# Two-layer graph network on one core: TensorE runs further ahead in the second layer, and the first layer's additions stand two groups later

## The reference, cut to what matters

```python
    edge_index = jnp.stack([src, dst])
    h = jnp.maximum(_layernorm(x, axis=-1), 0.0)
    x = x + _L0_gnn_ref(h, edge_index, L0_gnn_kernel, L0_gnn_bias)
    h = jnp.maximum(_layernorm(x, axis=-1), 0.0)
    x = x + _L1_gnn_ref(h, edge_index, L1_gnn_Wq, L1_gnn_bq, L1_gnn_Wk, L1_gnn_bk, L1_gnn_Wv, L1_gnn_bv, L1_gnn_gamma, L1_gnn_beta)
```

```python
        sums = jax.ops.segment_sum(msg, row, num_segments=n)
        cnt = jax.ops.segment_sum(jnp.ones_like(ew), row, num_segments=n)
        reduced = sums / jnp.maximum(cnt, 1.0)[:, None]
        h = jnp.concatenate([reduced, x], axis=1) @ kernel + bias
        return jax.nn.relu(h)
```

```python
        att = jnp.einsum('ehd,ehd->eh', q, k) / jnp.sqrt(jnp.float32(HEAD_DIM))
        exp_att = jnp.exp(jnp.clip(att, -10.0, 10.0))
        att_sum = jax.ops.segment_sum(exp_att, rows, num_segments=num_nodes)
        att_norm = exp_att / (att_sum[rows] + 1e-08)
        weighted_v = (att_norm[..., None] * v).reshape(-1, D_MODEL)
        out = jax.ops.segment_sum(weighted_v, rows, num_segments=num_nodes)
```

## Time and profile before

| | us |
|---|---|
| median of 3 runs | 6205.74 (6203.47 to 6215.74) |
| the profiled execution | 6258.93 |
| its span | 6257.2 |
| PE busy | 3015.3 (48%) |
| DVE busy | 3094.1 (49%) |
| ACT busy | 1816.7 (29%) |
| POOL busy | 3185.1 (51%) |

### The profile page before, as it was taken

How to read it: one execution, slowest core, us unless ns; L and a number is a source line. 1 busy time by engine, 2 the same in 40 slices (tenths; PEclk the granted TensorE clock), 3 DMA queues, 4 the chain that set the end, 5 groups by cost and what they waited for, 6 DMA issues and landing times. The chain is left out here.

```text
span 6257.2 us, 86473 instructions
## 1 busy us (share of the span) xinstructions
PE 3015.3 (48%) x21028; PEld 2368.1 (38%) x21028; DVE 3094.1 (49%) x8514; ACT 1816.7 (29%) x5489; POOL 3185.1 (51%) x3338
## 2 busy tenths in 40 slices
PE   4445445445445445344465555554554545445453
PEld 3323323333333233233243444444444444444442
DVE  6536445445445445344244555555555555555556
ACT  3233332333332333333443222222222222222222
POOL 4364464464463464554535555555555555555554
PEclk8555555556556555555557666666666666666666
DMA  2231231231222221222322222222222222222223
GB/s 80 54 82 47 64 82 46 67 79 48 70 74 50 73 73 49 76 70 62 73 54 75 76 75 75 76 76 76 76 76 76 76 76 75 76 76 75 75 76 56
DMA packets 205061, 436.91 MB, mean 70 GB/s; under 512 B 67172, under 2 KB 114781, under 8 KB 204606
## 3 DMA queue, kind: packets, MB, share of 16 engines
q0 software_dynamic: 153968, 371.50, 22.4%
q1 hardware_dynamic: 49934, 59.56, 3.4%
q10 hardware_dynamic: 704, 0.33, 0.0%
HBM read 415.27 MB, written 55.69 MB: 75 GB/s over the span
## 5 line engine op out<-in xcount | busy, mean ns | idle before, releaser
L525 POOL DMA_INDIRECT got<-hk_table,dst x1563 | 1523.3, 975 | 1513.1 <-PE bank L1000 821.5
L1486 POOL DMA_INDIRECT kv<-kv_table,dst_i x1611 | 1527.0, 948 | 1287.6 <-DVE wv_s L1528 846.8
L766 DVE TENSOR_TENSOR acc<-acc,bank 128x129 f32 x2187 | 635.3, 290 | 1480.8 <-remote 737.7
L1633 PE MATMUL bank<-q,ohT 128*128 x4833 | 617.9, 281 | 934.5 <-ACT ohT L1585 834.0
L998 PE MATMUL bank<-got,oh 128*128 x2187 | 616.9, 285 | 794.5 <-issue 445.1
L1644 PE MATMUL bank<-wv_s,oh_f 128*128 128x136 f32 x3222 | 768.5, 397 | 463.9 <-DVE wv_s L1528 249.8
L1507 DVE TENSOR_TENSOR prod<-bank,kv 128x384 f32<-128x384 f32 x537 | 297.7, 554 | 1271.6 <-remote 1042.3
L1633 PEld LDWEIGHTS bank<-q,ohT 128*128 128x128 bf16 x4833 | 481.7, 121 | 1035.1 <-issue 985.8
L1644 PEld LDWEIGHTS bank<-wv_s,oh_f 128*128 128x128 f32 x3222 | 635.2, 279 | 536.0 <-DVE wv_s L1528 297.9
L1579 ACT ACTIVATE oh_f<-oh 128x384 f32<-128x384 bf16 x537 | 279.6, 521 | 1683.0 <-remote 1235.2
L1101 ACT ACTIVATE oh<-away 128x384 bf16<-128x384 bf16 x733 | 383.8, 524 | 1311.5 <-remote 788.0
(11 more groups left out here) (223 smaller groups left out, 3409.3 us busy)
## 6 DMA issues: line engine op xcount, KB each, us to landing
slots_by_bin<-sorted_chunk SPq DMA_DIRECT2D x637, 61.0 KB
kv<-kv_table,dst_i POOLq DMA_INDIRECT x1611
got<-hk_table,dst POOLq DMA_INDIRECT x1563
kv_table<-qkv SPq DMA_DIRECT2D x12, 512.0 KB, 2.9
hk_table<-hk POOLq DMA_DIRECT2D x6, 772.0 KB, 5.7
out<-o SPq DMA_DIRECT2D x12, 256.0 KB
xs<-in_x SPq DMA_DIRECT2D x3, 768.0 KB, 10.7
sorted_chunk<-vT SPq DMA_DIRECT2D x13, 64.0 KB
```

The lines of the kernel that those rows point to most:

```text
L525: g.indirect_dma_start(out=got[:, (tile0[k] + t) % RING0, :], out_offset=None, in_=hk_d, in_offset=bass.IndirectOffsetOnAxis(dst0[:, k % 2 ...
L766: v.tensor_tensor(out=o, in0=o, in1=bank[5 + u % 3][:, i * W0:(i + 1) * W0], op=ALU.add)\
L1486: g.indirect_dma_start(out=kv[:, r, i, :], out_offset=None, in_=kv_d, in_offset=bass.IndirectOffsetOnAxis(dst_i[:, t:t + 1], 0))\
L1633: ins = t.matmul(bank[2 + u % 2][:, i * D:(i + 1) * D], ohT[:, u % 2, i * P:(i + 1) * P], q3[:, bass.ds(regs[0][(s + i) % REGS], 1), j * D ...
```

## The change

In the second layer all distances of PE grow by one or two groups: the transposes stand 4 groups ahead instead of 2, the queries 3 instead of 1, and the sums 2 behind instead of 1. PSUM's banks are shared anew: the transposes have one bank (0) instead of two, the queries three (1 to 3) instead of two, the sums keep two (4, 5). The one-hot matrices on DVE are made 5 groups ahead instead of 3, the widening and the eviction on ACT stand 4 ahead instead of 2, and the buffers `oh_f`, `ohT` and `wv_s` are twice as deep. DVE's additions stay 3 groups behind. In the first layer DVE adds the group two earlier (`LAG0`), with the placing steps where they were; the last two groups are added behind the loop.

```diff
@@ first layer, DVE
+                groups = [(i, g) for i in range(CHUNKS) for g in range(groups0(i))]
                 for k in range(1, CHUNKS + 1):
...
-                        if g < groups0(k - 1):
-                            add(k - 1, g)
+                        if g < groups0(k - 1) and group0[k - 1] + g >= LAG0:
+                            add(*groups[group0[k - 1] + g - LAG0])
...
+                for k, g in groups[-LAG0:]:
+                    add(k, g)
@@ second layer, buffers
-        oh_f = sbp(phase, "oh_f", [P, 4, G, P], FP32)
-        ohT = sbp(phase, "ohT", [P, 2, G * P], BF16)
+        oh_f = sbp(phase, "oh_f", [P, 8, G, P], FP32)
+        ohT = sbp(phase, "ohT", [P, 4, G * P], BF16)
...
-        wv_s = sbp(phase, "wv_s", [P, 2, G, W], FP32)
+        wv_s = sbp(phase, "wv_s", [P, 4, G, W], FP32)
@@ DVE, weigh
-                    if u >= 2:
-                        v.wait_ge(s_s, u - 1)
+                    if u >= 4:
+                        v.wait_ge(s_s, u - 3)
@@ DVE, the loop
-                    if u + 3 < GROUPS:
-                        hot(u + 3)
+                    if u + 5 < GROUPS:
+                        hot(u + 5)
@@ ACT, widen and the loop
-                    if u >= 4:
-                        a.wait_ge(s_s, u - 3)
+                    if u >= 8:
+                        a.wait_ge(s_s, u - 7)
...
-                    if u + 2 < GROUPS:
-                        widen(u + 2)
-                        evict(u + 2)
+                    if u + 4 < GROUPS:
+                        widen(u + 4)
+                        evict(u + 4)
@@ PE, turn
-                    if u >= 2:
-                        t.wait_ge(s_oT, u - 1)
+                    if u:
+                        t.wait_ge(s_oT, u)
@@ PE, queries
-                    if u >= 2:
-                        t.wait_ge(s_prod, u - 1)
+                    if u >= 3:
+                        t.wait_ge(s_prod, u - 2)
@@ PE, the loop
-                for u in range(GROUPS + 1):
-                    if u + 2 < GROUPS:
-                        turn(u + 2)
-                    if u + 1 < GROUPS:
-                        queries(u + 1)
-                    if u:
-                        sums(u - 1)
+                for u in range(GROUPS + 2):
+                    if u + 4 < GROUPS:
+                        turn(u + 4)
+                    if u + 3 < GROUPS:
+                        queries(u + 3)
+                    if u >= 2:
+                        sums(u - 2)
```

More of the change, by code:

```diff
@@ L1525, in weigh @@
                     v.wait_ge(s_exp, u + 1)
[L1526 to L1528 removed]
+                    if u >= 4:
+                        v.wait_ge(s_s, u - 3)
+                    v.tensor_tensor(out=by_head(wv_s[:, u % 4, :, 0:D]),
                                     in0=by_head(kv[:, u % RING1, :, D:2 * D]),
@@ L1549, in _ @@
                 v.wait_ge(s_i1, 1)
-                for u in range(3):
+                for u in range(5):
                     hot(u)
@@ L1576, in widen @@
                     a.wait_ge(s_o1, u + 1)
-                    if u >= 4:
-                        a.wait_ge(s_s, u - 3)
-                    a.activation(oh_f[:, u % 4, :, :], oh1[:, u % 4, :, :], ACT.Copy).then_inc(s_of, 1)
+                    if u >= 8:
+                        a.wait_ge(s_s, u - 7)
+                    a.activation(oh_f[:, u % 8, :, :], oh1[:, u % 4, :, :], ACT.Copy).then_inc(s_of, 1)
                 def evict(u):
                     a.wait_ge(s_tt, u + 1)
-                    if u >= 2:
-                        a.wait_ge(s_q, u - 1)
-                    a.activation(ohT[:, u % 2, :], bank[u % 2][:, :].bitcast(BF16)[:, 0:G * P], ACT.Copy)\
+                    if u >= 4:
+                        a.wait_ge(s_q, u - 3)
+                    a.activation(ohT[:, u % 4, :], bank[0][:, :].bitcast(BF16)[:, 0:G * P], ACT.Copy)\
                      .then_inc(s_oT, 1)
@@ L1591, in expo @@
                         a.wait_ge(s_wgh, u)
-                    if u >= 2:
-                        a.wait_ge(s_s, u - 1)
-                    a.activation(wv_s[:, u % 2, :, D:W], att[:, u % 2, :, :], ACT.Exp,
+                    if u >= 4:
+                        a.wait_ge(s_s, u - 3)
+                    a.activation(wv_s[:, u % 4, :, D:W], att[:, u % 2, :, :], ACT.Exp,
                                  scale=float(HEAD_DIM) ** -0.5)
@@ L1597, in expo @@
                      .then_inc(s_exp, 1)
-                for u in range(2):
+                for u in range(4):
                     widen(u)
@@ L1643, in sums @@
                     for i in range(G):
-                        ins = t.matmul(bank[4 + u % 2][:, i * W:(i + 1) * W], oh_f[:, u % 4, i, :],
-                                       wv_s[:, u % 2, i, :], start=True, stop=True)
+                        ins = t.matmul(bank[4 + u % 2][:, i * W:(i + 1) * W], oh_f[:, u % 8, i, :],
+                                       wv_s[:, u % 4, i, :], start=True, stop=True)
                     ins.then_inc(s_s, 1)
                 turn(0)
-                turn(1)
-                queries(0)
-                for u in range(GROUPS + 1):
-                    if u + 2 < GROUPS:
-                        turn(u + 2)
-                    if u + 1 < GROUPS:
-                        queries(u + 1)
-                    if u:
-                        sums(u - 1)
+                for u in range(3):
+                    turn(u + 1)
+                    queries(u)
+                for u in range(GROUPS + 2):
[5 more added lines that the diff above has]
+                        sums(u - 2)
     layer1.close()
```

9 lines of the change are left out of this document (4 added, 5 removed).

## The result

The changed kernel takes 6119.35 us (median of 4 runs, 6104.86 to 6125.97) against 6210.54 (6203.47 to 6215.74) for the kernel before: ratio 0.9851, 95% interval 0.9829 to 0.9872. It is 91 us faster; 6444 had been forecast, slower. The time lies in the stated range of 6030 to 6590, but only because that range was drawn down to rival A's end; the forecast's own range was 6260 to 6590. It lies near rival A's 6095.

What follows compares the result with a forecast made beforehand. It took the second layer to be bound by a ring of waits in which PE's signals are held while gathers land. The median 6205.74 plus 263 (second layer) minus 25 (first layer) gave 6444 us, range 6030 to 6590, its own 6260 to 6590.

Steps and rivals of the forecast that it cites:

- rival A: Second layer: sums slip through, rounds keep three groups and only the restart is shorter; −86, 6095 us; chance 0.15.
- What bounds the kernel: Second layer: while a train's gathers land, PE's signals are held and come together 2.97 us after its last gather.
- Step 2: Second layer: queries 3 ahead take away the product's 1042 us wait, but only as far as DVE's additions allow.
- Step 3: Second layer: sums lose one iteration of slack and are held, so rounds carry two groups instead of three; +263 us.
- rival B: Second layer: signals late by a fixed delay, hidden by look-ahead, POOL the bound; −809, 5372 us; 0.13 with what lies toward A.
- Step 1 and 4: Second layer: transposes 4 ahead in one bank, taken as 0; deeper buffers opening the held sum's detour, 0 beside the round.
- First layer: First layer: additions two groups later let placing work fill DVE's waits for sums; −25 us, bounds −91 to +123.
- two upper bounds, +387 and +123: Second layer if the restart stays at 2.60 us, +387; first layer if PE's waits for additions double, +123.

Runs made afterwards that it cites:

- a1_second: The change's second layer alone, with the first layer's additions as in the kernel before: 4594.67 us, ratio 1.0001, on a chip with prompt signals.
- c1_lag1: The kernel before with the first layer's additions one group behind, old second layer: 6176.83 us, ratio 0.9935, on the chip with held signals.
- d3: Changed second layer with sums one behind, old first layer, each PE signal passed through a small DMA: 4815.34 us, ratio 1.0487 to the kernel before.
- d4: Changed second layer with sums two behind, old first layer, each PE signal passed through a small DMA: 5065.37 us, ratio 1.1024 to the kernel before.
- a2_first: The change's first layer alone, all second-layer edits undone: 4559.38 us, ratio 0.9916 to the kernel before, prompt signals.
- b2_adds4: The changed kernel with second-layer additions 4 groups behind instead of 3, three banks for sums, two for queries: 4559.48 us, ratio 0.9915 to the kernel before.
- a3_sums1: The changed kernel with the second layer's sums one group behind instead of two: 4554.89 us, ratio 0.9918 to the kernel before, prompt signals.
- a4_deep: The kernel before with only the deeper buffers, all distances unchanged: 4596.96 us, ratio 1.0003, prompt signals.

## Why the prediction was wrong, point by point

**What bounds the kernel: right for its chip, but for one reading.** Trains of nine gathers, held signals, a release 3 us after the last gather: all is in the trace after as in the one before. That the held signals "come together" is not so: in the earlier trace rows the held sums pass at 5007.03, 2.2 us before the product's signal, and over all trains the fourth signal comes at a median of 10.7 us into the train, the fifth at 12.9. As a statement on gathers it is too wide: on chips with prompt signals the same rows land without a pause and PE's signals are never late. There the Trainium skill's rule (SBUF — State Buffer, section Who interferes with whom) and the trace agree: in a1_second PE's signals come at a median of 0.01 us after the modelled end while rows land. On the chip with held signals no run tells whether the rule fails or something else holds the signals. Nor does a run tell whether the signals alone are late or the matmuls too, since a matmul's recorded end is modelled.

**Step 2, the queries' look-ahead: right.** The product's wait is gone (1042.3 to 2.5 us), DVE stands at the addition at the release, and POOL starts 2.13 us after it instead of 2.60. These are single rounds: times the 179 rounds of nine gathers the 0.47 us make 84 us, close to the 86 that the second layer gained, and partly by luck. The mean over all trains is 2.55 us before (and in c1_lag1) and 2.15 after, 0.40 us or some 70 us in all; the rest is that the release comes a little sooner, by the mean 3.07 us after the last gather in c1_lag1 and 2.96 us after it in the changed kernel.

**Step 3, the sum's lost iteration: the wait was right, the price was wrong, and this is the step that failed.** The wait at the additions came (1169 us), but not its price: −86 us were measured in the second layer where +263 had been forecast. The price of 263 us rested on "3.4 is nearer to the held one, so I take them as held": sums that end 3.4 us after the train's start were taken as held, because in the earlier trace rows sums that ended at 4.13 were. In the round above they end 3.75 us after the start (4745.89 + 1.70 against 4743.84), and the addition at 4748.15 follows 0.56 us later. In another round of the changed kernel they end 5.13 us after the start, later than the held ones of the earlier trace rows, and still pass within 0.2 us:

```profile
4758.94 0.95 POOL L1491 DMA_INDIRECT kv<-kv_table,dst_i  x1 [4.14 <-DVE wv_s L1533]
...
4762.37 1.70 PE L1649 MATMUL bank<-wv_s,oh_f 128*128 128x136 f32 x6
...
4764.21 0.30 DVE L1551 TENSOR_TENSOR acc<-acc,bank 128x136 f32 x1 [1.91 <-issue]
```

So the time from the train's start does not decide. (The profile marks this wait "issue", since the record of this signal is missing; the addition starts 0.14 us after the sums' end.) What both traces have in common is a count. Over all trains of the loops, the first three PE signals after a train's start come at medians of 1.53, 1.85 and 4.27 us before, and at 0.77, 2.22 and 4.21 us after; the fourth comes at 10.7 us before and 7.1 after, the fifth at 12.9 and 12.8. Before, the order was sums, transposes, queries, and the fourth, the sums, were held. After, it is transposes, queries, sums: the sums are third and pass. The trains one by one say the same (all ends of PE's work here are the recorded, modelled ones). Before, the signal of these sums came 3.5 us or more after their end in all of 171 trains, also in the 29 in which they ended within 3.75 us of the train's start. After, the addition starts within 1 us of their end in 170 of 172 trains, also in all 22 in which they ended later than 4.5 us. But the count is not strict: the third signal before is itself 1.5 us late by the median, and in c1_lag1, with the old order, the fourth is only 4.2 us late by the median and in 6 of 171 trains under 1 us. DVE gets its third `weigh` of the round (4749.48), so the train stays at nine. What is held now is the transposes (the eviction at 4750.89, 2.98 us after their end) and the second group of queries and sums, and for the transposes and queries there is look-ahead. That three signals pass per train is read from the traces of two orders; no run tested it, for instance by another order of PE's three operations on this kind of chip, and why it is so stays open.

**That the sum lost an iteration of slack is true,** and shown under another condition: with a plain delay on every signal it costs 250 us (d3 against d4, prompt signals), and the new order loses to the old one by 161 us on the chip with held signals. There the mechanism of the forecast is right, and rival B's, that a longer look-ahead hides a plain delay, is wrong for this order.

**Rival A** had the round within 0.03 us (15.13 against 15.10), the second layer's −86, and the time within 25 us (6095 against 6119); what it missed is the first layer's term. It had 0.15 as its chance. Its condition, that an end 3.4 us into the train is still prompt, came true; but so is an end at 5.1 us. Rival A and the forecast both sought an edge in microseconds, and none fits the two traces.

**Step 1 and 4:** transposes in one bank cost next to nothing here (PE waits 33.8 us for evictions there, 17.2 of them once); with a delayed signal the rows of d3 point at the single bank. The deeper buffers alone do nothing on prompt chips; on the other kind they were not measured.

**First layer: −25 forecast.** On chips with prompt signals it is −35 to −40 (a2_first, b2_adds4, a3_sums1); on the chip with held signals about −2 by the traces, inside the stated bounds. The upper bound's way is seen beside the gain's: PE waits for additions 722 us instead of 246.5, while DVE's remote wait fell from 705.2 to 642.3 us.

**Against the profiled execution** the sum inherited another flaw: the trace of before was 53 us above its median, and 24 us of that lay in the second loop, if c1_lag1's trace is taken as the usual one (2812.5 against 2788.3). The upper end of the forecast's range, 6590, also leaves out that its two upper bounds, +387 and +123, can come together (6716); nothing hung on that here.

## What to carry to other kernels

When signals are held up in bursts, ask which operation stands where in the engine's sequence when the burst begins, and not only at what microsecond it ends; a shift of the order by one operation can decide which wait is met. Look-ahead on one operand moves a wait to the next operand: here 1265 us at the product reappeared as 1169 at the additions, and most of the gain was that the restart got shorter. Price both directions of a distance: with two groups DVE waited less for PE and PE more for DVE, POOL's wait ended above where it had begun, and in the first layer one group was the better choice on the kind of chip of the result.

## What the runs showed of the hardware that was not expected

The same kernel takes 6210 us on one chip and 4594 us on another, with a gather's issue and DVE's operations equally long (a gather 0.949 and 0.946 us) and with PE's signals late on the first alone: 6.7 us in the earlier trace rows, and by the medians some 8 us for the fifth of a train. The granted clock differs too, 0.62 against 0.69 by the mean of the runs of before; one matmul of the queries takes 281 ns before and 267 in a4_deep, the same order on the other kind. That is 5% on PE's matmuls, against 35% in the time. The gain of a change can belong to one kind of chip: this one's second layer is worth 86 us or nothing.

On the chip with held signals, a relay that delays each of PE's signals by a DMA made the old order 94 us faster (0.9846). Its trains are shorter, mostly six gathers; why the restart then comes sooner no run shows.
